# Loading the input a second time, pixels on the partitions, in a fused kernel of four image blocks

## The reference

```
q = x.reshape(B, C, H * W)
energy = jnp.einsum('bcn,bdn->bcd', q, q)
energy_new = jnp.max(energy, axis=-1, keepdims=True) - energy
attention = jax.nn.softmax(energy_new, axis=-1)
out = jnp.einsum('bcd,bdn->bcn', attention, q)
pooled = concatenate([x, out], axis=1).mean(axis=(2, 3))
se = sigmoid(relu(pooled @ w1.T + b1) @ w2.T + b2)
x1 = se * x + (1.0 - se) * out
```

## Time and profile before

| what | value |
|---|---|
| median of 3 runs | 530.28 us (529.22 to 533.23) |
| the profiled execution | 526.66 us |
| its span, first to last instruction | 524.9 us |
| mean granted clock of TensorE | 0.954 of full |
| busy: PE, PEld, DVE, ACT, POOL | 455.3, 354.0, 351.0, 263.0, 136.0 us |
| instructions | 10106 |

### The profile page before, as it was taken

One profiled execution on the slowest core, in us unless ns is written; L12 is line 12 of the kernel. 1 busy time (PEld: TensorE's weight loads), 2 busy tenths in 40 slices (PEclk: granted clock), 3 DMA queues, 4 the chain that ended last, 5 costly groups with the idle time before them and its releaser, 6 DMA issues.

```text
span 524.9 us, 10106 instructions
## 1 busy us (share of the span) xinstructions
PE 455.3 (87%) x3522; PEld 354.0 (67%) x3522; DVE 351.0 (67%) x895; ACT 263.0 (50%) x654; POOL 136.0 (26%) x161
## 2 busy tenths in 40 slices
PE   4286786889999999999999999989988998785995
PEld 3163564467777768776776877677676788784885
DVE  1416856686769677877867786687466345675996
ACT  3321764555555364645555554535534514994540
POOL 6220375152104102210221131021111012503662
PEclk9996798979999999999999999999997999996999
DMA  5000111100000000000000000000000000004111
GB/s 218 20 8 15 38 34 30 55 21 22 1 1 22 21 1 20 20 0 0 20 20 0 0 20 0 1 21 2 0 4 19 1 22 2 0 1 160 42 56 64
DMA packets 9486, 13.15 MB, mean 25 GB/s; under 512 B 496, under 2 KB 8816, under 8 KB 9328
## 3 DMA queue, kind: packets, MB, share of 16 engines
q1 hardware_dynamic: 9456, 12.76, 7.2%
HBM read 8.56 MB, written 4.19 MB: 24 GB/s over the span
## 4 chain that ended last, share of the span: by engine, by line
PE 56%; DVE 20%; ACT 9%; issue 8%; POOL 4%; DMA 2%; DVEq 1%; SPq 0%; ACTq 0%; POOLq 0%
PE bank L1199 7%; PE bank L1312 5%; PE bank L1201 5%; PE bank L1200 5%; PE bank L1394 5%; PE bank L1368 4%; PE bank L1366 2%; PE bank L1344 2%; DVE nmax L992 2%; PE bank L1217 2%; PE bank L1422 2%; PE bank L1381 2%; ACT x L798 2%; DVE even L892 2%; DMA w_stage<-convs 1%
## 5 line engine op out<-in xcount | busy, mean ns | idle before, releaser
L1199 PE MATMUL bank<-win,w_hi 128*128 128x256 f32 x384 | 121.6, 317 | 12.4 <-DVE win L1145 5.9
L1201 PE MATMUL bank<-win,w_lo 128*128 128x256 f32 x384 | 109.1, 284 | 0.0
L1200 PE MATMUL bank<-win,w_hi 128*128 128x256 f32 x384 | 109.1, 284 | 0.0
L740 ACT ACTIVATE prob<-bank 128x512 f32<-128x512 f32 x128 | 69.6, 597 | 75.3 <-PE bank L1366 74.5
L992 DVE TENSOR_REDUCE nmax<-bank 128x2 f32<-128x512 f32 x128 | 85.2, 683 | 18.5 <-PE bank L1344 18.1
L1199 PEld LDWEIGHTS bank<-win,w_hi 128*128 128x128 f32 x384 | 73.5, 191 | 23.7 <-issue 10.8
L1200 PEld LDWEIGHTS bank<-win,w_hi 128*128 128x128 f32 x384 | 73.7, 192 | 0.5
L1201 PEld LDWEIGHTS bank<-win,w_lo 128*128 128x128 f32 x384 | 73.5, 191 | 0.0
L517 POOL TENSOR_TENSOR first<-first 128x256 f32<-128x256 f32 x24 | 17.7, 737 | 163.7 <-ACT first L629 163.7
L1368 PE MATMUL bank<-qk 32*128 32x256 f32 x256 | 41.3, 339 | 4.4 <-ACT prob L740 3.9
L1368 PEld LDWEIGHTS bank<-qk 32*128 32x128 f32 x256 | 24.8, 191 | 18.1 <-issue 5.6
(11 more groups left out here) (235 smaller groups left out, 924.3 us busy)
## 6 DMA issues: line engine op xcount, KB each, us to landing
w_stage<-convs SPq DMA_DIRECT2D x4, 576.0 KB, 3.8
x_in<-x SPq DMA_DIRECT2D x8, 256.0 KB, 2.6
out<-x_pair SPq DMA_DIRECT2D x8, 256.0 KB, 2.2
q<-out SPq DMA_DIRECT2D x1, 2048.0 KB, 8.2
out<-v SPq DMA_DIRECT2D x8, 256.0 KB, 2.1
cst<-small SPq DMA_DIRECT2D x1, 1708.0 KB, 8.7
cst<-small SPq DMA_DIRECT2D x1, 253.5 KB, 3.0
```

The lines of the kernel that those rows point to most:

```text
L740: act.activation(prob[:, x // 4 % 2, x % 4, :, :], bank[ST_BANK[x % 2]][:, :], ACT.Exp, scale=L2_SCALE).then_inc(st_exp, 1)
L1199: mm(dst, hi, x_hi, start=(row == 0), stop=False)
L1200: mm(dst, hi, x_lo, start=False, stop=False)
L1201: return mm(dst, lo, x_hi, start=False, stop=(row == KH - 1))
```

## The change

The DRAM side gets a second copy of the input, `x_px`, laid out on the host as pixel, image, chunk, channel. SP loads a pair of it straight into x_t, in place of PE's four transposes and ACT's copy; the steps "xt" are gone from the tables. The first load of x_t stands ahead of all other loads. In `load_x` the load of x_t waits for energy_done, the one of x_in for the rest, as before. Energy on PE takes over the waits of "xt" (for z0_exp and qk_low), with xt_loaded for the data; "o0" gets the wait for x_loaded.

```diff
--- before.py
+++ after.py
@@ -59,11 +59,11 @@
 L3_SCALE = float(1.0 / np.sqrt(np.float32(C)))
 FAR = -1e30
 
-EARLY = ("xt", "sum_x", "energy", "e_min", "att0", "att0_inv", "att0t", "o0", "diff0", "hid0", "z0", "se", "x1", "red",
+EARLY = ("sum_x", "energy", "e_min", "att0", "att0_inv", "att0t", "o0", "diff0", "hid0", "z0", "se", "x1", "red",
          "taps0", "taps1", "taps2")
-PE_SLOTS = {"xt": 2, "hid1": 3, "z1": 4, "energy": 4, "xht": 5, "dft": 7, "att0t": 7, "o0": 9, "dot1": 9, "even": 11,
+PE_SLOTS = {"hid1": 3, "z1": 4, "energy": 4, "xht": 5, "dft": 7, "att0t": 7, "o0": 9, "dot1": 9, "even": 11,
             "hid0": 13, "filt": 12, "z0": 14, "patt": 14, "y1": 15, "gsum": 17, "red": 19}
-ACT_SLOTS = {"xr": 0, "xt": 2, "sum_x": 3, "hid1": 3, "z1": 4, "att0": 6, "att0t": 7, "ab": 7, "o0": 11, "even": 11, "att1": 11,
+ACT_SLOTS = {"xr": 0, "sum_x": 3, "hid1": 3, "z1": 4, "att0": 6, "att0t": 7, "ab": 7, "o0": 11, "even": 11, "att1": 11,
              "hid0": 13, "filt": 13, "z0": 14, "red": 19}
 DVE_SLOTS = {"n2m": 1, "xh": 3, "xht": 5, "e_min": 5, "gate": 6, "att0_inv": 7, "logit1": 9, "att1_n": 12, "post_att": 14,
              "se": 16, "x2": 16, "x1": 17, "gvar": 17, "xn": 19, "taps0": 20, "taps1": 21, "taps2": 22}
@@ -125,7 +125,7 @@
 FIRST_W = AT["gw1"][0]
 
 
-def program(nc, x, small, convs, out):
+def program(nc, x, x_px, small, convs, out):
     with ExitStack() as ctx:
         def sb(name, shape, dt=F32):
             return ctx.enter_context(nc.sbuf_tensor(name, shape, dt))
@@ -304,7 +304,7 @@
         pool_set, vec_set, vec_pre, bias_mm = sem("pool_set"), sem("vec_set"), sem("vec_pre"), sem("bias_mm")
         bn_pow, table_loaded = sem("bn_pow"), sem("table_loaded")
 
-        xt_done, xt_copied, energy_done, e_min_done = sem("xt_done"), sem("xt_copied"), sem("energy_done"), sem("e_min_done")
+        xt_loaded, energy_done, e_min_done = sem("xt_loaded"), sem("energy_done"), sem("e_min_done")
         att0_exp, att0_inv_done, att0t_done, att0t_copied = sem("att0_exp"), sem("att0_inv_done"), sem("att0t_done"), sem("att0t_copied")
         o0_done, o0_scaled, diff0_done, sum_x_done = sem("o0_done"), sem("o0_scaled"), sem("diff0_done"), sem("sum_x_done")
         hid0_done, hid0_relu, z0_done, z0_exp = sem("hid0_done"), sem("hid0_relu"), sem("z0_done"), sem("z0_exp")
@@ -405,6 +405,7 @@
 
         @block.sync
         def _(sp):
+            sp.dma_start(x_t[:, :, :, :], x_px[:, 0:2, :, :]).then_inc(xt_loaded, 16)
             sp.dma_start(x_in[:, :, :], x_d[:, 0:2, :]).then_inc(x_loaded, 16)
             sp.dma_start(cst[:, 0:FIRST_W], small[:, 0:FIRST_W]).then_inc(cst_loaded, 16)
             sp.dma_start(cst[:, FIRST_W:], small[:, FIRST_W:]).then_inc(cst2_loaded, 16)
@@ -415,7 +416,8 @@
                 sp.dma_start(w_stage[:, :], convs[:, k * 3 * KC:(k + 1) * 3 * KC]).then_inc(wst_loaded, 16)
 
             def load_x(i):
-                sp.wait_ge(xt_done, i)
+                sp.wait_ge(energy_done, i)
+                sp.dma_start(x_t[:, :, :, :], x_px[:, bass.ds(2 * i, 2), :, :]).then_inc(xt_loaded, 16)
                 sp.wait_ge(o0_done, i)
                 sp.wait_ge(sum_x_done, i)
                 sp.wait_ge(diff0_done, i)
@@ -630,10 +632,6 @@
                                ACT.Copy).then_inc(first_copied, 1)
 
             def stage(what, i):
-                if what == "xt":
-                    act.wait_ge(xt_done, i + 1)
-                    act.activation(x_t[:, :, :, :].rearrange("p m k c -> p (m k c)"), bank[0][:, :],
-                                   ACT.Copy).then_inc(xt_copied, 1)
                 if what == "sum_x":
                     act.wait_ge(x_loaded, 16 * i + 16)
                     for m in range(2):
@@ -1201,17 +1199,10 @@
                 return mm(dst, lo, x_hi, start=False, stop=(row == KH - 1))
 
             def stage(what, i):
-                if what == "xt":
-                    pe.wait_ge(x_loaded, 16 * i + 16)
+                if what == "energy":
+                    pe.wait_ge(xt_loaded, 16 * i + 16)
                     after(pe, z0_exp, i)
                     after(pe, qk_low, 4 * (i - 2) + QUADS)
-                    for m in range(2):
-                        for q in range(CH):
-                            o = (m * CH + q) * C
-                            ins = tr(bank[0][:, o:o + C], x_in[:, m, q * P:(q + 1) * P], ident)
-                    ins.then_inc(xt_done, 1)
-                if what == "energy":
-                    pe.wait_ge(xt_copied, i + 1)
                     for m in range(2):
                         for q in range(CH):
                             ins = mm(bank[0][:, m * C:(m + 1) * C], x_t[:, m, q, :], x_t[:, m, q, :],
@@ -1224,6 +1215,7 @@
                     ins.then_inc(att0t_done, 1)
                 if what == "o0":
                     pe.wait_ge(att0t_copied, i + 1)
+                    pe.wait_ge(x_loaded, 16 * i + 16)
                     for m in range(2):
                         ins = mm(bank[0][:, m * HW:(m + 1) * HW], att0_t[:, m, :], x_in[:, m, :], start=True, stop=True)
                     ins.then_inc(o0_done, 1)
@@ -1676,12 +1668,13 @@
     for k, (b, e) in AT.items():
         small[:t[k].shape[0], b:e] = t[k]
     convs = _np.concatenate([a["L3_conv_W" + k].transpose(1, 3, 2, 0).reshape(C, TAPS * C) for k in "qkvc"], 1)
-    arrays = {"x": _np.ascontiguousarray(a["x"]), "small": small, "convs": _np.ascontiguousarray(convs)}
+    x_px = a["x"].reshape(N, C, CH, P).transpose(3, 0, 2, 1)
+    arrays = {"x": _np.ascontiguousarray(a["x"]), "x_px": _np.ascontiguousarray(x_px), "small": small, "convs": _np.ascontiguousarray(convs)}
 
     nc = _bacc.Bacc("TRN2", target_bir_lowering=False, num_devices=1, dynamic_dma_scratch_size=1024)
     ap = {k: nc.dram_tensor(k, v.shape, _mybir.dt.from_np(v.dtype), kind="ExternalInput").ap()
           for k, v in arrays.items()}
     out = nc.dram_tensor("out", _OUT[0], _mybir.dt.from_np(_np.dtype(_OUT[1])), kind="ExternalOutput").ap()
-    program(nc, ap["x"], ap["small"], ap["convs"], out)
+    program(nc, ap["x"], ap["x_px"], ap["small"], ap["convs"], out)
     r = _run(nc, [arrays], core_ids=[0])
     return r.results[0]["out"]
```

## The result

The changed kernel takes 537.62 us in the median of 4 runs (536.63 to 541.0); the kernel before, timed beside it, 531.02 us (529.22 to 533.23). The ratio is 1.0134, with a 95% interval of 1.0071 to 1.0196. The forecast of 529.8 us and its range are missed, on the slow side.

A forecast was written before the change was run, and what follows sets the result against it. PE was taken as the bound, busy 43.63 of 45.00 us in the steady part. +0.43 - 0.48 + 0 - 0.40 + 0 = -0.45 us, off the median 530.28, gave 529.8 us; range 526.4 to 533.5.

The forecast's parts named there:

- Pair 3: Near 104 to 106 us: without transposes and copy, L1252 and the energy matmuls start earlier, -0.40 us (bounds -1.2 and 0).
- a slow stretch there: Rival, faster: PE's slow stretch between 108 and 120 us falls away, -3.8 us, giving 526.4; chance 0.08.
- The rival of a falling clock: Without transposes the clock falls at 149 to 152 us in the loop: 3.4 us each, 533.2 to 543.4; chance 0.07.
- Its sign: What would show the clock falling in the loop: a PEclk digit under 9 between 175 and 380 us.
- The loop, 0: Pairs 4 to 7: PE would wait about 0.76 us for DVE's join instead of transposing, so nothing gained; bound -2.4.
- The rival of the full price: The four loop transposes count 0.60 us each: together -2.9 us (527.4), or -5.3 (525.0) with ACT's copies; chance 0.08.
- The head, +0.43: Pair 0: the new first load delays the weights by 0.64 us, so x1 starts 0.43 us later; bounds +0.29, +0.68.
- The rival of the second load: The second new load, issued at 7.5 us, takes another 0.64 us from w_stage: 530.4 to 530.5; chance 0.05.
- Pair 1, -0.48: ACT's x_t copy at 25.15 us stands in a serial chain; without it, -0.48 us.
- Pair 2, 0: Between 57 and 85 us the convolution weights' chain sets the end, so time saved on PE and ACT gains 0.
- SP's queue: The new wait holds nothing up; loop loads have some 41 us of slack, so loads disturb only the first 12 us.
- the rival of a late load: Loop loads of x_t take 43 us, beyond their slack: +2 us in each of four, +8, 538; chance 0.01.

The follow-up runs named there:

- a_tr2: The changed kernel with four unread transposes put back on PE for the third image pair (pair 2) only: 536.13 us, ratio 1.0073 to the kernel before.
- a_tr3: The changed kernel with four unread transposes put back on PE for pair 3 only: 530.11 us, ratio 1.0005 to the kernel before.
- b_loads: The kernel before with the added loads of x_t, whose data ACT's copy then overwrites; transposes stay: 531.77 us, ratio 1.0022.
- a_products: The changed kernel with unread ordinary products with the identity on PE where the transposes of each pair stood: 531.58 us, ratio 0.9945.

## Why the prediction was wrong, by its steps

- **Pair 3 is the step that failed.** It gave -0.40 us: the transposes stand in a wait and cost nothing, so what goes is ACT's copy. The wait was read rightly, but the transposes were taken for free cover, and what else they did in the gap wasn't priced. Without them PE idles 1.31 us and not 0.72, the clock falls at the gap, and a second fall follows it: 4.8 us in the two passes (a_tr2 against a_tr3), and 2.7 in the tail, whose cause stays open. The prediction even named a slow stretch there, and as a gain alone: "pair 3's step moves it", 526.4 us. It should have asked the same of both signs.
- **The rival of a falling clock had the mechanism and the wrong place.** It looked for the fall in the loop, where PE is busy for 97% of the time. It never came there: 1.00 in 300 to 345 us. The place was the passes ahead of the loop, where the kernel before already had slow stretches. Its price was nearly right: two falls at 3.4 us each give 536.6 us, and the median is 537.6. Its sign came true too, a PEclk digit of 7 at about 363 us, though behind the loop.
- **The loop, 0: right.** A pass is 47.4 us long as before. In the changed kernel at 160 us the convolution waits for the join:

```profile
159.87 0.75 DVE L1032 TENSOR_TENSOR k<-first,bank 128x256 f32 x2
...
160.67 0.38 PE L1197 MATMUL bank<-win,w_hi 128*128 128x256 f32 x1 [0.75 <-DVE k L1032]
```

  0.75 us of wait, 0.76 forecast. The rival of the full price falls with it.
- **The head, +0.43: right in kind, too small.** The changed kernel in order of time:

```profile
5.75 2.05 PE L1208 MATMUL bank<-x_t 128*128 128x128 f32 x8
...
13.12 0.99 POOL L468 TENSOR_TENSOR v<-w_stage 128x384 f32<-128x384 f32 x1 [3.90 <-DMA w_stage<-convs]
...
17.57 0.88 DVE L878 SCALAR_TENSOR_TENSOR x<-diff,se,o 128x256 f32<-128x256 f32 x2 [2.02 <-POOL diff L488]
```

  Energy starts at 5.75 us and not at 5.35, and x1 at 17.57 and not at 17.04, +0.96 against the earlier trace rows, released by POOL's diff0 as said. The weights were 10.4 us under way and were issued 0.4 us later, 1.12 us in all against 0.64 in the sum: the queues moved 301 GB/s in 6 to 7 us, not 410. The bound of 0.89 us, from the mean rate, was nearer. The rival of the second load, issued at 7.84 us while the weights were under way, doesn't explain it: in b_loads that load is issued at 11.48 us, and POOL's first mix still starts at 13.00 against 13.12.

```profile
6.00:7.00 1.00, 1.00 (x6) 1.00 (x7) 0.45 (x3) 0.28 (x1) 1.00 (x2) 1.00 0.83 301
```

- **Pair 1, -0.48: right.** Its gate matmul starts 0.47 us later than before and its energy 0.48, against 0.96 - 0.48. **Pair 2, 0: not contradicted**; the spread of the clock's rise covers a term of this size.
- **SP's queue and the second load: right.** x_t of pair 4 is issued at 117.59 us, ahead of the loop, and no wait of PE in the loop is put down to it. The eight loads of x_t landed after 2.7 to 5.9 us, so the rival of a late load, at 43 or 51 us, is far off. (The 2.7 us from which its 51 were worked out is a plain load's, and not that of the crossbar, to which the factor of 19 belongs.)

## What to carry to other kernels

PE work in an idle gap can be what keeps the clock up: before taking it away, look at the granted clock around each gap that grows, above all near the stretches that are already slow, and price a fall there for both signs. Where a small change costs far more than its own instructions, put the removed work back unread, a piece at a time; it tells in one comparison whether the result of the work or its mere presence mattered. And look at the whole trace: the clock can fall far behind the change, in code that is the same in both kernels. Here that made 2.7 us of the loss, and it happened in some kernels that weren't late at all.

## What the runs showed of the hardware that was not expected

- Where PE's idle time in pair 3's gap was 1.31 us, and not 0.72 or less, the granted clock fell from 2.4 to 1.2 GHz, in seven traces of seven; eight 128x128 matmuls then took 2.08 us instead of 1.16. The length of the wait alone doesn't decide: one of 1.34 us at 118.31 us of the changed kernel left the clock at 1.00.
- Unread products made a kernel faster: 9 of them, with one reorder of loads that alone changed nothing (1.0002), gave 0.9889.
- The granted clock of the first stretch isn't what the rows say: the page's first slices stand at 9 and 6 to 7 us at 1.00, before and after, while the eight energy matmuls take 2.08 and 2.05 us there, the time at the lower level. Only a_products has records so early, and it shows 0.50 from 12.4 to 36.2 us. Ahead of the first recorded change of the clock, go by the durations.
- The first two loads of 256 KB into x_t landed after 3.0 and 5.9 us, the eight of them after 3.0 in the median; the same size into x_in after 2.8 in the first 20 us and 2.6 in the median.
